# Fused attention and expert layer on one core: slot computation one group later, token scatters in the next step, token and slot buffers kept twice, two transposes of the maxima two slots later

## The reference

```
x = x + attention(layernorm(x))     # 16 heads of 16, rotary positions, causal softmax
x = x + moe(layernorm(x))           # 8 experts, top 2 of each token, hidden 1024

# moe, for each batch:
top_k_logits, expert = top_k(h @ router_w + router_b, 2);  prob = softmax(top_k_logits)
pos   = running count of the tokens that chose this expert (all first choices, then all second)
buf[expert, pos] += h                # at most 153 places for each expert and batch
o[e]  = (silu((buf[e] @ w_fc + b_fc) * (buf[e] @ w_gate + b_gate))) @ w_proj + b_proj
out   = prob[0] * o[expert0, pos0] + prob[1] * o[expert1, pos1]
```

## Time and profile before

| | |
|---|---|
| median of 3 runs | 1281.28 us (1278.86 to 1283.59) |
| profiled execution | 1272.76 us, span 1271.0 us, mean granted clock 0.975 |
| PE busy (matmuls) | 1176.4 us, 93% of the span |
| DVE / POOL / ACT busy | 731.0 / 689.9 / 483.7 us |
| attention phase, steps 2 to 6 | 63.1 to 63.4 us a step, PE busy 60.4 to 60.5 us |
| step 7, until the first maxima transpose of step 8 | 50.6 us, PE busy 49.5 us |
| from there to expert 0's second block of rows (519 to 607 us) | 88.0 us, PE busy 72.9 us |
| rest of the expert phase (607 to 1271 us) | 664.0 us, PE busy 632.6 us |

### The profile page before, as it was taken

How to read it: one execution, slowest core, us unless ns; L and a number is a source line. 1 busy time by engine, 2 the same in 40 slices (tenths; PEclk the granted TensorE clock), 3 DMA queues, 4 the chain that set the end, 5 groups by cost and what they waited for, 6 DMA issues and landing times.

```text
span 1271.0 us, 24010 instructions
## 1 busy us (share of the span) xinstructions
PE 1176.4 (93%) x8264; PEld 1002.1 (79%) x8264; DVE 731.0 (58%) x1523; ACT 483.7 (38%) x988; POOL 689.9 (54%) x976
## 2 busy tenths in 40 slices
PE   4699999999999999878999999999999999999992
PEld 3466767666767676578899999999999999999982
DVE  6677787878787867755343433343433333435664
ACT  2145454545454545533333322333332233332320
POOL 4234335353535343577567655566666555767634
PEclk9699999999999999989999999999999999999996
DMA  4876745454545455343121121131211221205345
GB/s 136 219 240 189 236 118 166 118 166 121 162 122 161 121 145 127 136 138 101 63 68 59 60 71 67 65 109 59 68 59 62 75 70 64 101 26 175 100 148 177
DMA packets 83134, 148.24 MB, mean 117 GB/s; under 512 B 9647, under 2 KB 60728, under 8 KB 78910
## 3 DMA queue, kind: packets, MB, share of 16 engines
q1 hardware_dynamic: 65344, 111.37, 30.5%
q0 software_dynamic: 7936, 26.60, 6.4%
q10 hardware_dynamic: 9728, 8.67, 2.2%
HBM read 93.05 MB, written 53.61 MB: 115 GB/s over the span
## 4 chain that ended last, share of the span: by engine, by line
PE 48%; issue 2%; POOL 1%; DMA 1%; DVE 0%; POOLq 0%; DVEq 0%; ACT 0%
PE ps L77 47%; PE ps L1307 1%; POOL wp_lo L1635 1%; POOL wp_hi L1635 0%; DMA raw<-x_rows 0%; DMA wp_lo<-slot_outputs,row_of 0%; DVE raw L1504 0%; DVE xl L1375 0%; POOLq L1655 0%; DVE ah L1463 0%; DVE gated L1532 0%; DVE al L1472 0%; DVEq L1655 0%; DVE o_sb L1519 0%; POOLq L1635 0%
## 5 line engine op out<-in xcount | busy, mean ns | idle before, releaser
L1570 POOL TENSOR_TENSOR al<-hid,ah 128x384 fp32r<-128x384 f32 (+1 forms) x168 | 179.3, 1067 | 210.8 <-DVE ah L1463 210.8
L1424 ACT ACTIVATE fc<-ps,b_fc 128x384 f32<-128x384 f32 (+1 forms) x192 | 115.5, 602 | 447.6 <-PE ps L77 445.3
L1532 DVE SCALAR_TENSOR_TENSOR gated<-ps,b_gate,fc 128x384 f32<-128x384 f32 (+1 forms) x192 | 123.3, 642 | 227.3 <-PE ps L77 211.8
L824 DVE TENSOR_REDUCE mx<-ps 128x2 f32<-128x256 f32 (+3 forms) x256 | 205.9, 819 | 36.6 <-PE ps L437 34.8
L437 PE MATMUL ps<-kst,qst 65*128 65x256 f32 (+2 forms) x512 | 148.5, 373 | 11.1 <-DMA kst<-qk_parts 11.1
L606 ACT ACTIVATE probs<-ps 128x512 f32<-128x512 f32 (+1 forms) x256 | 123.1, 538 | 55.3 <-PE ps L455 54.4
L1519 DVE TENSOR_TENSOR o_sb<-ps,b_proj 128x256 f32<-128x256 f32 x80 | 33.9, 424 | 156.8 <-PE ps L77 156.8
L598 ACT ACTIVATE probs<-ps 128x256 f32<-128x256 f32 (+1 forms) x128 | 62.6, 490 | 136.2 <-PE ps L449 135.3
L958 POOL TENSOR_TENSOR rope_c<-qk_b,rope_table 128x512 f32<-128x512 f32 x32 | 43.0, 1344 | 125.7 <-ACT qk_b L634 125.6
L1392 ACT ACTIVATE hid<-gated 128x384 f32<-128x384 f32 (+1 forms) x192 | 102.7, 535 | 6.9 <-DVE gated L1532 6.9
L77 PE MATMUL ps<-xh,wg_hi 128*128 128x384 f32 (+1 forms) x384 | 103.4, 350 | 2.1 <-DVE gated L1532 2.1
(11 more groups left out here) (188 smaller groups left out, 2468.5 us busy)
## 6 DMA issues: line engine op xcount, KB each, us to landing
qk_parts<-hilo SPq DMA_DIRECT2D x32, 512.0 KB, 3.1
qst<-qk_parts SPq DMA_DIRECT2D x64, 256.0 KB, 4.9
kst<-qk_parts SPq DMA_DIRECT2D x64, 256.0 KB, 5.5
slot_tokens<-zeros POOLq DMA_DIRECT2D x12, 816.0 KB, 5.9
rows<-slot_tokens SPq DMA_DIRECT2D x24, 384.0 KB, 3.6
slot_outputs<-o_sb SPq DMA_DIRECT2D x72, 128.0 KB, 1.7
raw<-in_wf SPq DMA_DIRECT2D x8, 1024.0 KB, 5.4
raw<-in_wg SPq DMA_DIRECT2D x8, 1024.0 KB, 7.4
```

Source lines behind the costliest of these rows:

```text
L824: V.reduce_max(mx[:, g % 2, 2 * pr:2 * pr + 2, i], both[:, :, 0:P * (i + 1)], AXX)\
L1424: A(fc[:, hc % 2, 0:width], ps[:, FC + hc % 2, 0:width], ACT.Identity, bias=b_fc[:, e, hc:hc + 1]).then_inc(fc_out, 1)
L1532: V.scalar_tensor_tensor(gated[:, hc % 2, 0:width], ps[:, GATE + hc % 2, 0:width], b_gate[:, e, hc:hc + 1], fc[:, hc % 2, 0:width], ALU.ad ...
L1570: G.tensor_tensor(al[:, at, 0:width], hid[:, hc % 2, 0:width], ah[:, at, 0:width].bitcast(F32), ALU.subtract).then_inc(al_done, 1)
```

## The change

What it does:

- DVE computes the slots at (3, 1) in place of (2, 1), in steps 2 to 7. In step 8 and for the last batch they stay at (2, 1).
- POOL issues the 8 scatters of a step's tokens in the next step's slots (0, 5), (0, 6), (0, 7) and (1, 0), two each, for steps 2 to 7. So step 8 has those of step 7 and its own; step 2 has none.
- `hn` and `put_at` are kept twice, by the parity of the step; `st_tok` becomes two semaphores. DVE waits for the scatters of two steps ago before it writes `put_at`. The second `hn` lies over the raw projection weights at the start and over more of `wp_lo` of the second expert in the expert phase, so POOL waits for all scatters at (2, 0) of expert 0 in place of (2, 4).
- SP waits, before it loads the first rows of expert 0, until the scatters of steps 2 to 7 have landed; the last of these now stand in step 8.
- The maxima's transposes (M) of groups 1 and 2 move from slots (1, 0) and (2, 0) to (1, 2) and (2, 2); ACT's copy and SP's send follow them one slot behind. Those of groups 0 and 3 stay.

```diff
-        hn = late.take("hn", [P, TT, C])
+        hn = Region(nc, (late.at - 4 * CK * C * 2, late.end)).take("hn", [P, 2, TT, C])
-        put_at = kept.take("put_at", [P, TT * K], I32)
+        put_at = kept.take("put_at", [P, 2, TT * K], I32)
...
-            (1, 0): ("M", 0), (1, 1): ("Q", 0), (1, 3): ("A", 0), (1, 4): ("Q", 1), (1, 5): ("F", 0),
+            (1, 1): ("Q", 0), (1, 2): ("M", 0), (1, 3): ("A", 0), (1, 4): ("Q", 1), (1, 5): ("F", 0),
...
-            (2, 0): ("M", 0), (2, 1): ("Q", 3), (2, 3): ("A", 0), (2, 4): ("V", 0), (2, 5): ("T", 0),
+            (2, 1): ("Q", 3), (2, 2): ("M", 0), (2, 3): ("A", 0), (2, 4): ("V", 0), (2, 5): ("T", 0),
...
+        M_AT = tuple(next(u for gg, u in PIECES if gg == g and PIECES[gg, u][0] == "M") for g in range(NG))
...
+        def slots_at(b):
+            return (3, 1) if b < BATCH else (2, 1)
+        SCATTER_NEXT = ((0, 5), (0, 6), (0, 7), (1, 0))
+        SCATTER_LAST = ((2, 1), (2, 3), (2, 4), (2, 6))
...
-                if u == 1 and piece_there(b, g, "M"):
+                if u == M_AT[g] + 1 and piece_there(b, g, "M"):
                     send_max(b, g)          # and so for ACT's max_out
...
+                wait(dve, st_tok[b % 2], 16 * 8 * ((b - 2) // 2))
+                V.tensor_tensor(put_at[:, b % 2]...
...
-                if (g, u) == (2, 1) and there(b, 2, 9):
+                if (g, u) == slots_at(b) and there(b, 2, 9):
                     slots(chain, b, 1)
...
-                    wait(dve, st_tok, 16 * 8 * (b - 1))
-                    wait(dve, hT_done, 2 * (b - 1))
-                    normalise(hn, x1, mv2, rs2, h_done)
+                    wait(dve, st_tok[(b - 1) % 2], 16 * 8 * ((b - 1) // 2))
+                    wait(dve, hT_done, 2 * (b - 2))
+                    normalise(hn[:, (b - 1) % 2], x1, mv2, rs2, h_done)
...
-                if (g, u) in SCATTER_AT and there(b, 2, 9):
+                if (g, u) in SCATTER_NEXT and there(b, 3, BATCH):
                     for n in range(2):
-                        scatter(b, 2 * SCATTER_AT.index((g, u)) + n)
+                        scatter(b - 1, 2 * SCATTER_NEXT.index((g, u)) + n)
+                if (g, u) in SCATTER_LAST and there(b, BATCH, 9):
+                    for n in range(2):
+                        scatter(b, 2 * SCATTER_LAST.index((g, u)) + n)
...
-            sp.wait_ge(rt["h_done"], BATCH - 1)
+            for landed in rt["st_tok"]:
+                sp.wait_ge(landed, 16 * NB * (BATCH // 2 - 1))
             load_rows(0, 0, 0)
```

More of the change, by code:

```diff
@@ L205, in attention_phase @@
         ld_max = sem("ld_max")
-        st_zero, st_tok = sem("st_zero"), sem("st_tok")
+        st_zero = sem("st_zero")
+        st_tok = rt["st_tok"] = [sem(f"st_tok{i}") for i in range(2)]
         made, z_ready = sem("made"), sem("z_ready")
@@ L514, in piece @@
                     wait(pe, h_done, b - 1)
-                    turn(misc, lambda k: hn[:, k, bass.ts(n, P)], TT).then_inc(hT_done, 1)
+                    turn(misc, lambda k: hn[:, b % 2, k, bass.ts(n, P)], TT).then_inc(hT_done, 1)
                 elif kind == "L":
@@ L775, in slots @@
                 chain(V.tensor_copy(rt["slot"][:, bass.ts(b - 2, TT * K)], slot_f[:].rearrange("p t k -> p (t k)")))
-                V.tensor_tensor(put_at[:].rearrange("p (t k) -> p t k", k=K), slot_f[:], over[:], ALU.add)\
+                wait(dve, st_tok[b % 2], 16 * 8 * ((b - 2) // 2))
+                V.tensor_tensor(put_at[:, b % 2].rearrange("p (t k) -> p t k", k=K), slot_f[:], over[:], ALU.add)\
                     .then_inc(put_done, 1)
@@ L939, in rsqrt @@
                 G.tensor_tensor(y, y, a, ALU.mult).then_inc(done, 1)
-            SCATTER_AT = ((2, 1), (2, 3), (2, 4), (2, 6))
             NEWTON = 13
@@ L986, in scatter @@
                     wait_apart(pool, put_done, b - 1, pool_passed)
-                G.indirect_dma_start(out=rt["tok"], out_offset=bass.IndirectOffsetOnAxis(ap=put_at[:, n:n + 1], axis=0),
-                                     in_=hn[:, n // K, :], in_offset=None, bounds_check=NSLOT - 1, oob_is_err=False)\
-                    .then_inc(st_tok, 16)
+                G.indirect_dma_start(out=rt["tok"], out_offset=bass.IndirectOffsetOnAxis(ap=put_at[:, b % 2, n:n + 1], axis=0),
+                                     in_=hn[:, b % 2, n // K, :], in_offset=None, bounds_check=NSLOT - 1, oob_is_err=False)\
+                    .then_inc(st_tok[b % 2], 16)
             def fill(n):
@@ L1272, in body @@
                         sp.wait_ge(turned, 2)
-                        sp.wait_ge(rt["st_tok"], 16 * NB * BATCH)
+                        for landed in rt["st_tok"]:
+                            sp.wait_ge(landed, 16 * NB * BATCH // 2)
                         load_rows(e2, n2, side(par, n + 1))
@@ L1593, in body @@
                                     pool.wait_ge(rt["st_x1"], 16 * BATCH)
-                                if (n, hc) == (2, 4):
-                                    pool.wait_ge(rt["st_tok"], 16 * NB * BATCH)
+                                    for landed in rt["st_tok"]:
+                                        pool.wait_ge(landed, 16 * NB * BATCH // 2)
                             if hc == 0:
```

## The result

The changed kernel takes 1271.65 us (median of 5 runs, 1269.73 to 1275.63) against 1282.51 us for the kernel before in the same sitting. The medians differ by 10.9 us. The ratio of the two is estimated as 0.9934, with a 95% interval of 0.9908 to 0.9960, which is some 8.5 us; the text goes by this. Forecast were 1278.1 us and 3.2 us. The profiled execution has a span of 1267.9 us and a mean granted clock of 0.969, against 1271.0 and 0.975: the two profiles are only 3.1 us apart.

What follows compares the result with a forecast made beforehand. PE, busy 93% of the span, was taken to bound the kernel. The terms -4.8 - 2.7 + 0.5 + 0.8 + 3.0 gave -3.2 us, so 1281.28 became 1278.1 us; own range 1275 to 1280.5, wide range 1272.5 to 1284.5.

Steps and rivals of the forecast that it cites:

- faster by more: Outcome under 1274.9 us, faster by more than the 0.5% (6.4 us) that can't be told from none; chance 0.22.
- same: Outcome with a difference under 0.5% (6.4 us), which can't be told from none; chance 0.71.
- Slots leave group 2: Group 2, steps 2 to 6: without slots, `xr` holds the rotary sum instead; gain 0.96 us a step, 4.8 in all.
- Transposes of the maxima: M at (1, 0) no longer waits for DVE's copy: gain 2.7 us over steps 0 to 6; nothing at (2, 0).
- Slots in group 3: Slots mostly fit DVE's wait for PE before the residual sum: cost 0.1 us a step, 0.5 in all.
- Scatters in groups 0 and 1: Eight scatters just fit POOL's idle time but can delay DVE: cost 0.2 us in steps 3 to 6, 0.8 in all.
- Step 8 and expert 0: Eight more scatters make POOL 5.0 us late, delaying `al` and the last `hn`: cost 3.0 us; first rows 0.2 late.
- The signs: Trace checks, including group 2 at 15.7 to 16.1 us, steps of 61.8 to 62.1, `hn` 2 to 4 us later.
- sign of "wrong": Steps still 63 us, rotary product late in group 1, or step 8 to second rows unchanged or over 6 us longer.
- the lock only moves: Rival: scatters and splitting meet DVE in groups 0 and 3, group 2 gains least; +1.5 us, 1282.8 us, chance 0.15.
- The late POOL: Rival: POOL's lateness in step 8 is hidden by other slack; -6.2 us, 1275.1 us; hidden or better, chance 0.22.

Runs made afterwards that it cites:

- slots alone: Changed kernel with the two transposes of the maxima back at (1, 0) and (2, 0), leaving slots, scatters and doubled buffers; ratio 0.9953.
- the second trace: Changed kernel run and profiled again, unaltered; ratio 0.9937 against the kernel before.
- biases-first trace: Changed kernel with SP's loads of the first expert's two biases ahead of the wait for the landed scatters; ratio 0.9939.
- `xr` moved alone: Kernel before, with POOL adding the bias to the residual rows at (2, 4) in place of (2, 1); ratio 1.0097.

## Why the prediction was right or wrong

The direction was right. The size was not: some 8.5 us timed against 3.2. By the ratio the forecast's base of 1281.28 us becomes 1272.8, just inside the wide range (1272.5 to 1284.5) and outside the prediction's own of 1275 to 1280.5; the sitting's median of 1271.65 lies under both. So what came is "faster by more", which had 0.22, not "same", which had 0.71. By its steps:

- **Slots leave group 2.** Right in kind, a little small. The rotary sum is held 2.53 us and the wait of 1.24 is gone, as said. Group 2 gave 1.25 us (slots alone: 15.62 against 16.87), not 0.96, since the probabilities cost 0.34 and not 0.62. The 0.62 was read in step 4, where `dlt` took 0.44 us beside a scatter; in step 3 it took 0.16, and 0.28 is the whole difference.
- **Transposes of the maxima.** 0.53 to 0.57 a step against 0.4, for steps 2 to 6. Behind Q only M's weight load waits for ACT's copy, 0.27 us. Step 0 was to gain 0.3 us. It ended 1.0 us earlier in the profile shown, but 1.3 to 3.5 us later than in before's three traces (92.8 to 93.3) in seven of nine traces with M moved. That cost was no term of the sum.
- **Slots in group 3.** 0.07 to 0.08 a step, forecast 0.1. Right.
- **Scatters in groups 0 and 1.** 0.07 a step, forecast 0.2. Right in kind; POOL had 0.58 us left, not 1.
- **Step 8 and expert 0.** The mechanism was right (POOL late, then `al`, then `hn`), the size too small: `hn` is transposed 4.2 to 5.0 us later against the profile shown, not 3.0. `al` ends 46.3 to 46.4 us behind step 8's first M, as forecast (565.4 less 518.99). In the second trace `hn` starts 1.2 us behind it, near the "about 1" of the forecast, but its four instructions then take 3.21 us, where I had 1.6 to 2.95. In the profile shown ACT did not wait for `al`, and `hn` starts 2.2 us behind it, as PE itself was late: the first rows came 1.8 us late, not 0.2, since one scatter took 1.61 us beside DVE's cast and PE waited for `b_gate`, whose load goes out 0.94 us behind the rows'; and the clock was low until 547.3. The clock was no term of the sum. To PE's end the transition lost 6.6 to 6.9 us against the profile shown, 4.1 to 4.4 against before's second and 2.1 to 2.5 against its third trace.
- **The signs.** Right were the held rotary sum, both vanished waits, groups 0 and 1 and the residual sum. Group 2 (15.6 us) and the steps (61.56) came out just under their ranges. `hn` came later than the 2 to 4 us. One sign of "wrong" was there too: the stretch to expert 0's second block of rows is 6.4 us longer in the profile shown, where over 6 was to count against the prediction.
- **What the sum lacked.** Between the two profiles shown, steps 1 to 7 gave 8.8 us against 5.9 forecast, what lies before them 1.0 against 0.3, and the transition cost 6.9 against 3.0: the errors nearly cancel, so the two profiles differ by 3.1 us, almost the forecast, for the wrong sizes. That is luck. As far as the traces show, the timed gain is larger because the profile shown was no typical execution of the kernel before. I had seen that it lay 8.5 us under the median and took it for a shift common to both kernels. It is not: its clock was 0.975, where twelve timed runs of the next sitting had 0.965 to 0.969. Of 43 later ones four had 0.975 as well, and took 1271.9 to 1273.1 us: such executions come, but seldom. Three traces of the kernel before have 0, 2 and 4 lengthened groups, 2.8 us on the mean, and the change takes away the wait that they follow. On the mean of these three against the two traces of the changed kernel the parts are +0.5 (up to step 1's start), -11.6 (steps 1 to 7) and +4.4 (transition), together -6.7 us. With the biases-first trace as a third it is -5.1. So most of the 8.5 measured is accounted for, not all of it, and the traces are few. That the wait brings the lower clock is what 13 of 25 against 0 of 35, and step 1, point to; no experiment inserts such a wait alone, so it is not shown.

Of the rivals, "the lock only moves" came true elsewhere, in `xr` moved alone. The late POOL was not hidden, nor paid in full.

## What to carry over

A short, repeated wait of the busiest engine can cost more than itself: behind a wait of 1.24 us stood 1.3 to 1.6 us lost at the lower clock in 13 of 25 cases, and none of this is in a list of waits. So look at the granted clock behind each such wait, in more than one execution, before a profile is taken as the base of a sum. And an instruction that holds another engine is worth moving only with a look at what stands beside it at its new place.

## What the runs showed that was not expected

- A hold can fall on an instruction of four numbers a partition: `dlt` took 2.87 us beside `xr`, in place of 0.16. The Trainium skill (SBUF — State Buffer, section "SBUF: two separate sides") has DVE and GpSimd exclude each other on a common port pair for a whole instruction, where DVE's has two inputs in SBUF or runs in a mode that uses both ports. `dlt` has one input, so by that rule it would be the mode; no run here shows which. The trace agrees in part: `dlt` ended with `xr` at 330.9, but it had begun 0.45 us before `xr`, beside a scatter.
- `xr` itself takes 2.82 to 2.84 us at (2, 1) in steps 1 to 6, where the slot computation or the rotary sum stands beside it, and 2.33 to 2.42 elsewhere, beside `dlt` too.
- The execution that is profiled can differ from the timed ones by what the clock does: of one program, spans of 1271.0, 1276.9 and 1281.1 us.
